# A decoder layer on one Trainium2 core: the order of work at the start of cross-attention, on three engines

## The chip, the cores and the metric

The kernel runs on 1 core of a Trainium2 chip. A core has five engines with queues of their own, each in order: TensorE (PE; its weight loads are shown apart as PEld), VectorE (DVE), ScalarE (ACT), GpSimd (POOL) and SyncE (SP), which here only issues DMAs. ScalarE issues a few DMAs too. Engines wait for each other on semaphores alone. The metric is the device time of one execution in microseconds; lower is better.

## The reference

32 sequences of 128 tokens with 128 features pass a state-space mixer, cross-attention with 16 heads of 8 features over a context of 128 tokens, and a mixture of 16 experts, each with a residual sum and a layer norm behind it. The change touches the start of the middle part:

```python
x = _layernorm(x + mixer(x))
q, k, v = split_heads(x @ Wq + bq), split_heads(ctx @ Wk + bk), split_heads(ctx @ Wv + bv)
scores = einsum('bhqd,bhkd->bhqk', q, k) / sqrt(8)
scores = where(mask, -1e15, scores)
attn = softmax(scores)
x = _layernorm(x + merge(einsum('bhqk,bhkd->bhqd', attn, v)) @ Wo + bo)
x = _layernorm(experts(x))
```

## The kernel before

The sequences are worked in 8 groups of 4. The mixer, attention and the experts are three blocks of straight code per engine; between mixer and attention each engine jumps into the next block by itself, after all have arrived there. Everything in a block is ordered by hand: each engine's function is a list of steps, and each step begins with its semaphore waits.

Attention of one group needs the scores twice. First `scores` makes them by query on TensorE (banks SS0 and SS1), VectorE takes the maximum of each row (`maxima`), splits the negated maxima into three bf16 parts (`split_maxima`, four small operations, L1367 to L1373), TensorE transposes them (`max_rows`, L1563, into bank PO), ScalarE copies them out and stores them to DRAM (`store_max`, L1261 and L1265), and loads them back as extra rows of the stacked queries (`stack_max`, L1271). Then `scoresT` makes the transposed scores with the maxima subtracted (banks TT0 and TT1), ScalarE takes the exponential (`exps`, L1253), and `weigh` multiplies by the values and by ones. `both(g, ..., b, ..., p)` is the steady pair of steps: transposed scores of group g and first scores of group g + 1, for sequence b and half p of the heads. In `both` the transposed scores of a half group wait for its stacked maxima (`d_m`), and each first-score step waits for VectorE's maxima of the turn before it (`v_max`), since the banks are used again.

Group 0 has no group before it, so its first scores are made ahead of the loop by `first_scores`, for sequences 0 to 3 and p 0 and 1; these use TT0 and TT1 as well, and VectorE's `first_maxima` reads them. Both halves of group 0's maxima are transposed there by `max_rows(0, 0)` and `max_rows(0, 1)`.

Around this the next groups are prepared. For group 2: ScalarE rounds the context (`context_hi`, L196), GpSimd takes the rest (L1184), TensorE projects keys (`k_proj`, L254) and transposes x1 (`x1T`, L245), ScalarE evicts (`part_first`, L219, and `x1T_hi`), VectorE takes the rests (`part_rest`, L232, and `x1T_lo`, L212), TensorE projects queries (`q_proj`, L254), and GpSimd makes the third parts (`part_third`, L239). SyncE stores the parts to DRAM and loads them back as stacked rows (`store_parts`, `stacks`). The first scores of group 2 wait for those stacks.

The layer norm of the mixer's last group also falls here: VectorE's `statistics` (L131 and L135, four each), then GpSimd's `normalise_pool` (L141 to L148), then `biased(0)` (L1189). GpSimd does these ahead of its `head(0, ...)`, which holds the mask casts (L1179) and `part_third` of group 2. SyncE waits for that norm before it goes on to `loads(3)` and `store_parts(2)`.

Of the kernel before, what the change touches and what calls it, by code (L numbers as in the profile page):

```python
# [25 lines left out]
GS = 4  # L26
# [271 lines left out]
def mixer(nc, t, d, psum, a):  # L298

    with ExitStack() as ctx:  # L300
# [3 lines left out]
        def sem(name, n=1, by=1):  # L304
            return Sem(ctx, nc, name, n, by)
# [21 lines left out]
        half_dt = sb("half_dt", [P, NSEQ, HEADS])  # L327
        th = sb("th", [P, NSEQ, ROT])

        w_loaded, const = sem("w_loaded", 1, 16), sem("const")  # L330
        wprep = sem("wprep")


        expo = sb("expo", [P, 2, HEADS, P])
# [724 lines left out]
def attention(nc, t, d, psum, a, e):  # L1059
# [12 lines left out]
    with ExitStack() as ctx:  # L1072
# [172 lines left out]
        def _(act):  # L1245
# [10 lines left out]
            def store_max(g, par, half):  # L1256

                act.wait_ge(p_mt.sem, p_mt.at(g, half))
                act.wait_ge(d_ms[half].sem[1 - par], d_ms[half].at(g - 1, 1 - par))
                tok = slice(half * 2 * P, half * 2 * P + 2 * P)  # L1260
                act.activation(nmT[:, tok], PO[:, :].bitcast(BF16)[0:48, tok], ACT.Copy).then_inc(a_mt.sem, 1)  # L1261
                act.wait_ge(a_mt.sem, a_mt.at(g, half))
                act.sem_inc(act_passed, 1)
                act.wait_ge(d_m[half].sem[par], d_m[half].at(g - 2, par))
                act.dma_start(m_dram[par, half], nmT[:, tok]).then_inc(d_ms[half].sem[par], 16)  # L1265
# [54 lines left out]
            for b in range(GS):  # L1320
                act.activation(mask[:, 1, b, :, :].rearrange("p k t -> p (k t)"),
                               mask8[:, 1, b * KINDS * P:(b + 1) * KINDS * P], ACT.Copy).then_inc(g_mask.sem, 1)
            store_max(0, 0, 0)
            context_hi(act, a, 2, 0)
            stack_max(0, 0, 0)
            store_max(0, 0, 1)
            ahead(act, group)

# [1 line left out]
        def _(dve):  # L1330
# [55 lines left out]
            def head(g, par, left, before=None):  # L1386
# [6 lines left out]
                    part_rest(dve, a, g + 2, 1, PF)  # L1393
                if left:
                    maxima(g + 1, 0, (2, 3))
                if left >= 2:
                    x1T_lo(dve, a, g + 2, PO)
                if left:
# [48 lines left out]
            values(0, 0, U0)  # L1447
            dve.wait_ge(g_init, 10)
            values(1, 1, PF)
            statistics(dve, NG - 1, t["x1_res"], dve_passed, res, stats, mv)  # L1450
            head(0, 0, 4)
            dve.wait_ge(x1_out.sem, x1_out.at(NG - 1, 3))
            ahead(dve, group)
# [2 lines left out]
        def _(pe):  # L1456
# [171 lines left out]
            for b in range(2):  # L1628
                for p in range(2):
                    first_scores(b, p)  # L1630
            project_v(pe, t, a, 1, PF)
            max_rows(0, 0, (t["x1_res"].sem, t["x1_res"].at(NG - 1, 0)))
            stacked(0, 0, 1)
            for b in range(2, GS):
                for p in range(2):
                    first_scores(b, p)
            max_rows(0, 1, (a_mt.sem, a_mt.at(0, 0)))
            pe.wait_ge(g_init, 9)
            both(0, 0, 0, 4, 0)
            head_parts(0, 0, 4)  # L1640
            both(0, 0, 0, 4, 1)
            for g in range(NG):
# [497 lines left out]
```

## Time and profile before

| what | us |
| --- | --- |
| median of 3 runs | 602.16 (601.14 to 604.1) |
| the profiled execution, its own time | 599.92 |
| its span from first to last instruction | 598.2 |
| TensorE busy | 545.5 (91% of the span) |
| VectorE busy | 445.2 (74%) |
| ScalarE busy | 280.1 (47%) |
| GpSimd busy | 229.1 (38%) |
| mixer block ends, first attention scores start | 203.0, 207.3 |
| attention's loop, about | 228 to 404 |

A timeline row gives the start and the duration in microseconds, the engine, the line of the kernel, the operation with the tile it writes and those it reads, how many instructions were merged, and in brackets how long the engine had been idle before it and who ended that. ACTq and SPq are the queues that issue DMAs. The clock column of a table of stretches is the TensorE clock that was granted, as a share of 2.4 GHz.

### The profile page before, as it was taken

How to read it: one execution, taken by the hardware profiler on the slowest of the kernel's cores; microseconds unless marked ns; L12 is line 12 of the kernel's file. 1: busy time of each engine (PE TensorE's matmuls, PEld its weight loads, DVE VectorE, ACT ScalarE, POOL GpSimd, SP SyncE). 2: the span in 40 equal slices, each digit the busy share in tenths (PEclk: the TensorE clock that was granted, in tenths of full speed). 3: DMA queues.
4: the chain of work that ended last, by engine and by line, in shares of the span. 5: the costliest groups of instructions: out<-in, count | busy, mean ns of one | idle time of the engine just before them, and what ended most of it. 6: DMA issues, size and time to landing. Idle time of an engine off the chain costs nothing. (4 is left out here: it accounts for less than half of the span.)

```text
span 598.2 us, 17812 instructions
## 1 busy us (share of the span) xinstructions
PE 545.5 (91%) x6344; PEld 452.9 (76%) x6344; DVE 445.2 (74%) x1080; ACT 280.1 (47%) x556; POOL 229.1 (38%) x273
## 2 busy tenths in 40 slices
PE   5769999999999669999999999878999999999994
PEld 5748877787788547878778777767888888888883
DVE  3857877877798487778778787665796887877963
ACT  2358647756675316556556455533323323233220
POOL 2233546534753665244543546713022032131122
PEclk9979999999999958999999999998999999999998
DMA  7124232312332762654654455007246265165160
GB/s 217 38 99 124 76 97 75 122 53 90 102 119 65 200 184 77 185 143 128 173 149 122 136 142 168 7 5 177 65 115 143 63 150 132 60 164 128 38 157 18
DMA packets 55217, 67.42 MB, mean 113 GB/s; under 512 B 6705, under 2 KB 33104, under 8 KB 55152
## 3 DMA queue, kind: packets, MB, share of 16 engines
q1 hardware_dynamic: 52976, 63.58, 39.3%
q0 software_dynamic: 704, 1.92, 1.1%
q10 hardware_dynamic: 1472, 1.05, 0.8%
q8 instruction: 41, 0.67, 0.5%
q14 instruction: 24, 0.20, 0.1%
HBM read 49.26 MB, written 11.21 MB: 101 GB/s over the span
## 5 line engine op out<-in xcount | busy, mean ns | idle before, releaser
L1253 ACT ACTIVATE prob<-bank 128x512 f32<-128x512 f32 x128 | 69.4, 595 | 41.1 <-PE bank L1499 34.8
L2031 PE MATMUL bank<-xT_hl_c,w_up 128*128 128x512 f32 x288 | 85.9, 422 | 2.9 <-ACTq L67 2.9
L1948 ACT ACTIVATE sg<-bank 128x512 f32<-128x512 f32 x72 | 43.1, 598 | 95.2 <-PE bank L2031 89.7
L1349 DVE TENSOR_REDUCE nmax<-bank 128x4 f32<-128x512 f32 x112 | 71.9, 684 | 20.6 <-PE bank L1499 19.3
L2042 PEld LDWEIGHTS bank<-w_down,hid 128*128 128x128 f32 x576 | 73.9, 191 | 10.8 <-DVE hid L1988 3.7
L2042 PE MATMUL bank<-w_down,hid 128*128 128x128 f32 x576 | 76.4, 276 | 2.4 <-DVE res L124 1.5
L1489 PE MATMUL bank<-neg_i,mask 64*128 64x256 bf16 x512 | 52.1, 283 | 12.8 <-DMA q_stack<-q_scratch 4.3
L2031 PEld LDWEIGHTS bank<-xT_hl_c,w_up 128*128 128x128 f32 x288 | 50.2, 194 | 10.0 <-issue 3.1
L1988 DVE TENSOR_TENSOR hid<-gu,share 128x512 f32<-128x512 f32 x64 | 48.9, 763 | 6.0 <-DMA share<-cw_scratch 3.7
L1984 DVE TENSOR_TENSOR gu<-sg,bank_pair 128x512 f32<-128x512 f32 x48 | 32.8, 684 | 19.2 <-ACT sg L1948 13.2
L1747 POOL TENSOR_TENSOR xT_hl_c<-rest,xT_hl_c 128x512 fp32r<-128x512 f32 x7 | 9.0, 1285 | 94.4 <-ACT xT_hl_c L1728 94.4
L491 ACT ACTIVATE expo<-rows,neg_sums 128x128 f32<-128x128 f32 x128 | 40.7, 390 | 9.1 <-DVE mix L913 9.1
L141 POOL TENSOR_TENSOR rstd<-mv,norm_c 128x4 f32<-128x4 f32 x24 | 5.2, 216 | 99.9 <-DVE mv L135 60.1
L820 POOL TENSOR_TENSOR w_tok<-w_tok,prev 128x512 f32<-128x512 f32 x16 | 22.4, 1401 | 52.0 <-DMA prev<-xnext 42.2
L2031 PE MATMUL bank_pair<-xT_hl_c,w_up 128*128 128x512 f32 x144 | 41.1, 394 | 0.0
L1489 PEld LDWEIGHTS bank<-neg_i,mask 64*128 64x128 bf16 x512 | 16.8, 96 | 27.9 <-issue 13.2
L1543 PE MATMUL bank_pair<-prob,v_d 128*32 128x128 f32 x1024 | 34.4, 275 | 0.0
L1539 PE MATMUL bank_pair<-prob,ones_s 128*32 128x128 f32 x1024 | 34.4, 276 | 0.0
L436 PE MATMUL bank<-xhl,w_feat 128*128 128x512 f32 (+1 forms) x96 | 28.2, 429 | 5.3 <-DVE b_rot L869 5.2
L983 PE MATMUL bank_pair<-plain 96*128 96x256 f32 x192 | 29.4, 289 | 3.0 <-DVE mix L913 2.9
L2031 PEld LDWEIGHTS bank_pair<-xT_hl_c,w_up 128*128 128x128 f32 x144 | 27.1, 188 | 6.4
L983 PEld LDWEIGHTS bank_pair<-plain 96*128 96x128 f32 x192 | 25.3, 189 | 8.0 <-DVE mix L913 7.6
(217 smaller groups left out, 1175.2 us busy)
## 6 DMA issues: line engine op xcount, KB each, us to landing
share<-cw_scratch SPq DMA_DIRECT2D x64, 256.0 KB, 5.5
rows<-sum_rows_scratch SPq DMA_DIRECT2D x32, 256.0 KB, 3.5
k_stack<-k_scratch SPq DMA_DIRECT2D x32, 128.0 KB, 2.8
q_stack<-q_scratch SPq DMA_DIRECT2D x32, 128.0 KB, 2.9
prev<-xnext SPq DMA_DIRECT2D x16, 224.0 KB, 2.5
k_scratch<-k_part SPq DMA_DIRECT2D x16, 192.0 KB, 2.4
q_scratch<-q_part SPq DMA_DIRECT2D x16, 192.0 KB, 2.5
x<-xT_in SPq DMA_DIRECT2D x8, 256.0 KB, 8.6
```

Of the source, the lines that this page charges most:

```text
L491: act.activation(expo[:, b % 2, h, :], rows[:, b, h, :], ACT.Exp, bias=upto_s[:, bass.ds(g * GS + b, 1), h]).then_inc(s_exp.sem, 1)
L983: pe.matmul(bank[:, 0:2 * P], plain[:, par, 0, a, tok], bc(plain[:, par, 1, v, None, tok], [PLAIN, 2, P]), start=(n == 0), stop=False, ski ...
L1253: act.activation(prob[:, b % 2, ORDER[n], :, :], (TT0, TT1)[n % 2][:, :], ACT.Exp, scale=XD ** -0.5)\
L1349: dve.tensor_reduce(nmax[:, b, 4 * u:4 * u + 4], (SS0, SS1)[n % 2][:, :].rearrange("p (i k) -> p i k", i=4), AX_X, ALU.max, negate=True).t ...
L1489: pe.matmul(banks[j][:, :].rearrange("p (i h k) -> p i h k", i=4, h=2)[:, :, half, :], mask[rows, par, b, kind + ver, :], bc(neg_i[rows, N ...
L1539: mm = pe.matmul(U1[32 * u:32 * u + 32, 0:P], ones_s[:, 4 * b + i, :, :].rearrange("p r c -> p (r c)"), prob[:, b % 2, u, i, :], start=(b ...
L1543: mm = pe.matmul(U0[32 * u:32 * u + 32, b * P:(b + 1) * P], v_d[:, par, b, i * P + 32 * u:i * P + 32 * u + 32], prob[:, b % 2, u, i, :], s ...
L1948: act.activation(sg[:, k, :], GG[k][:, :], ACT.Silu).then_inc(a_s.sem, 1)
L1984: dve.tensor_tensor(dst, sg[:, k, :], UU[k][:, :], ALU.mult).then_inc(v_gu.sem, 1)
L1988: dve.tensor_tensor(hid[:, c, :], gu[:, k, :], share[:, c - 1, :], ALU.mult).then_inc(v_hid.sem, 1)
L2031: mm = pe.matmul(bank[:, :], w_up[:, which, a, c, :], xT_hl[par][:, v, :], start=(n == 0), stop=(n == 2))
L2042: mm = pe.matmul(PO[:, b * P:(b + 1) * P], hid[:, c, b * P:(b + 1) * P], w_down[:, c, :], start=(c == 0 and b == 0), stop=(c == NC - 1), s ...
```

## The change

Three engines' lists are reordered at the start of attention, and one step is moved on VectorE. No work is added or taken away. (Three semaphores of the mixer that nothing used are dropped as well, so that lines from there on are numbered two lower.)

- TensorE: `first_scores(2, 0)`, with the wait for the second half's stacks, goes ahead of `max_rows(0, 0)`. `max_rows(0, 1)` goes from ahead of `both(0, ..., 0)` to behind it. Ahead of `both` stands a wait for all 16 of group 0's maxima, which the wait in `max_rows(0, 1)` held before.
- ScalarE: `stack_max(0, 0, 0)` goes ahead of `context_hi(2)`.
- VectorE: `statistics` of the mixer's last group goes from ahead of `head(0, ...)` into it, behind the second pair of group 1's maxima and ahead of `x1T_lo(2)`.

```diff
--- before.py
+++ after.py
@@ -327,8 +327,6 @@
         half_dt = sb("half_dt", [P, NSEQ, HEADS])
         th = sb("th", [P, NSEQ, ROT])
 
-        w_loaded, const = sem("w_loaded", 1, 16), sem("const")
-        wprep = sem("wprep")
 
 
         expo = sb("expo", [P, 2, HEADS, P])
@@ -1321,8 +1319,8 @@
                 act.activation(mask[:, 1, b, :, :].rearrange("p k t -> p (k t)"),
                                mask8[:, 1, b * KINDS * P:(b + 1) * KINDS * P], ACT.Copy).then_inc(g_mask.sem, 1)
             store_max(0, 0, 0)
+            stack_max(0, 0, 0)
             context_hi(act, a, 2, 0)
-            stack_max(0, 0, 0)
             store_max(0, 0, 1)
             ahead(act, group)
 
@@ -1393,6 +1391,8 @@
                     part_rest(dve, a, g + 2, 1, PF)
                 if left:
                     maxima(g + 1, 0, (2, 3))
+                if not before:
+                    statistics(dve, NG - 1, t["x1_res"], dve_passed, res, stats, mv)
                 if left >= 2:
                     x1T_lo(dve, a, g + 2, PO)
                 if left:
@@ -1447,7 +1447,6 @@
             values(0, 0, U0)
             dve.wait_ge(g_init, 10)
             values(1, 1, PF)
-            statistics(dve, NG - 1, t["x1_res"], dve_passed, res, stats, mv)
             head(0, 0, 4)
             dve.wait_ge(x1_out.sem, x1_out.at(NG - 1, 3))
             ahead(dve, group)
@@ -1629,14 +1628,15 @@
                 for p in range(2):
                     first_scores(b, p)
             project_v(pe, t, a, 1, PF)
+            stacked(0, 0, 1)
+            first_scores(2, 0)
             max_rows(0, 0, (t["x1_res"].sem, t["x1_res"].at(NG - 1, 0)))
-            stacked(0, 0, 1)
-            for b in range(2, GS):
-                for p in range(2):
-                    first_scores(b, p)
-            max_rows(0, 1, (a_mt.sem, a_mt.at(0, 0)))
+            for b, p in ((2, 1), (3, 0), (3, 1)):
+                first_scores(b, p)
+            pe.wait_ge(v_max.sem, v_max.at(0, 4 * GS - 1))
             pe.wait_ge(g_init, 9)
             both(0, 0, 0, 4, 0)
+            max_rows(0, 1, (a_mt.sem, a_mt.at(0, 0)))
             head_parts(0, 0, 4)
             both(0, 0, 0, 4, 1)
             for g in range(NG):
```

TensorE's queue around the first transposes of maxima. L260 is the product of values (`project_v`); a row of L1489 and one of L1499 with k_stack first are a turn of first scores, with q_stack first a turn of transposed scores; L1563 is `max_rows`. Before:

```order
L260 MATMUL bank<-w_v,cin 128x128 x4
L1563 MATMUL bank<-ident,npart 48x128 x2
L1489 MATMUL bank<-neg_i,mask 128x4x64 x4
L1499 MATMUL bank<-k_stack,q_stack 128x128 x8
L1489 MATMUL bank<-neg_i,mask 128x4x64 x4
```

and in the changed kernel, where those lines are 1488, 1498 and 1562:

```order
L260 MATMUL bank<-w_v,cin 128x128 x4
L1488 MATMUL bank<-neg_i,mask 128x4x64 x4
L1498 MATMUL bank<-k_stack,q_stack 128x128 x8
L1562 MATMUL bank<-ident,npart 48x128 x2
L1488 MATMUL bank<-neg_i,mask 128x4x64 x4
```

The transposes now stand behind one more turn of first scores.

TensorE's queue some turns later, from the last first scores of group 0 to the second turn of `both`. Before:

```order
L1489 MATMUL bank<-neg_i,mask 128x4x64 x4
L1499 MATMUL bank<-k_stack,q_stack 128x128 x8
L1563 MATMUL bank<-ident,npart 48x128 x2
L1489 MATMUL bank<-neg_i,mask 128x4x64 x4
L1499 MATMUL bank<-q_stack,k_stack 128x128 x8
L1489 MATMUL bank<-neg_i,mask 128x4x64 x4
L1499 MATMUL bank<-k_stack,q_stack 128x128 x8
L254 MATMUL bank<-c_hl,wqk_hl 128x512 x3
L245 MATMUL bank<-ident,x 128x128 x4
L1489 MATMUL bank<-neg_i,mask 128x4x64 x4
```

and in the changed kernel:

```order
L1488 MATMUL bank<-neg_i,mask 128x4x64 x4
L1498 MATMUL bank<-k_stack,q_stack 128x128 x8
L1488 MATMUL bank<-neg_i,mask 128x4x64 x4
L1498 MATMUL bank<-q_stack,k_stack 128x128 x8
L1488 MATMUL bank<-neg_i,mask 128x4x64 x4
L1498 MATMUL bank<-k_stack,q_stack 128x128 x8
L1562 MATMUL bank<-ident,npart 48x128 x2
L254 MATMUL bank<-c_hl,wqk_hl 128x512 x3
L245 MATMUL bank<-ident,x 128x128 x4
L1488 MATMUL bank<-neg_i,mask 128x4x64 x4
```

The transposes of the second half's maxima have moved from ahead of the first turn of `both` to behind it, directly ahead of the keys' projection (L254) and the transposes of x1 (L245).

ScalarE's queue around the stored maxima, with its waits. Before:

```order
L1261 ACTIVATE nmT<-bank 48x256 [waits max_stored0_1,max_mm]
L1265 DMA max_scratch<-nmT 48x256 [waits nmT_ready,max_stacked0_0]
L196 ACTIVATE c_hl<-cin 128x512 [waits k_mm,ctx_in0]
L1271 DMA q_stack<-max_scratch 3x2048 [waits max_stored0_0]
L1271 DMA q_stack<-max_scratch 3x2048
L1261 ACTIVATE nmT<-bank 48x256 [waits max_stored1_1,max_mm]
L1265 DMA max_scratch<-nmT 48x256 [waits nmT_ready,max_stacked1_0]
```

and in the changed kernel:

```order
L1259 ACTIVATE nmT<-bank 48x256 [waits max_stored0_1,max_mm]
L1263 DMA max_scratch<-nmT 48x256 [waits nmT_ready,max_stacked0_0]
L1269 DMA q_stack<-max_scratch 3x2048 [waits max_stored0_0]
L1269 DMA q_stack<-max_scratch 3x2048
L196 ACTIVATE c_hl<-cin 128x512 [waits k_mm,ctx_in0]
L1259 ACTIVATE nmT<-bank 48x256 [waits max_stored1_1,max_mm]
L1263 DMA max_scratch<-nmT 48x256 [waits nmT_ready,max_stacked1_0]
```

The two loads of `stack_max`, which wait for the store of the maxima, now stand ahead of the context's copy (L196). The copy of the second half's maxima (L1261 before, L1259 now) is where it was, ahead of the loop's exponentials.

VectorE's queue from the values of group 1 to the first split of group 1's maxima. Before:

```order
L1341 TENSOR_TENSOR v_d<-bank,b_v 128x4x4x8 x4
L131 BN_STATS stats<-res 128x6 x4
L135 BN_AGGR mv<-stats 128x2 x4
L1349 TENSOR_REDUCE nmax<-bank 128x4 x2
L232 SCALAR_TENSOR_TENSOR rest<-bank,bqk,k_part 128x512
L1349 TENSOR_REDUCE nmax<-bank 128x4 x2
L212 TENSOR_TENSOR xT_hl<-bank,xT_hl 128x512
L1349 TENSOR_REDUCE nmax<-bank 128x4 x4
L1367 SCALAR_TENSOR_TENSOR npart<-nmax 128x4x8
```

and in the changed kernel:

```order
L1339 TENSOR_TENSOR v_d<-bank,b_v 128x4x4x8 x4
L1347 TENSOR_REDUCE nmax<-bank 128x4 x2
L232 SCALAR_TENSOR_TENSOR rest<-bank,bqk,k_part 128x512
L1347 TENSOR_REDUCE nmax<-bank 128x4 x2
L131 BN_STATS stats<-res 128x6 x4
L135 BN_AGGR mv<-stats 128x2 x4
L212 TENSOR_TENSOR xT_hl<-bank,xT_hl 128x512
L1347 TENSOR_REDUCE nmax<-bank 128x4 x4
L1365 SCALAR_TENSOR_TENSOR npart<-nmax 128x4x8
```

The eight operations of `statistics` have moved from ahead of the first pair of maxima to ahead of `x1T_lo` (L212) and the four maxima of sequence 1.

## Rows read from the trace of the kernel before

**Rows 1.** Stretch and length; busy of PE, PEld, DVE, ACT, POOL; clock, DMA, GB/s.

```profile
215.00:230.00 15.00, 9.74 (x111) 7.05 (x111) 12.32 (x33) 4.68 (x9) 8.15 (x10) 0.58 0.41 107
...
260.00:400.00 140.00, 133.25 (x3026) 108.71 (x3024) 105.54 (x269) 77.45 (x149) 69.58 (x80) 1.00 0.43 121
```

**Rows 2.** TensorE's timeline: start, duration (us), line, operation, count [idle before <-releaser].

```profile
222.97 0.38 PE L1563 MATMUL bank<-ident,npart 128*48 128x128 bf16 x2 [3.24 <-DVE npart L1373]
...
223.84 0.61 PE L1489 MATMUL bank<-neg_i,mask 64*128 64x256 bf16 x4 [0.50 <-issue]
...
225.66 1.65 PE L254 MATMUL bank<-c_hl,wqk_hl 128*128 128x512 f32 x3
...
227.90 0.39 PE L1489 MATMUL bank<-neg_i,mask 64*128 64x256 bf16 x4
...
229.80 0.40 PE L1489 MATMUL bank<-neg_i,mask 64*128 64x256 bf16 x4 [0.84 <-ACT prob L1253]
...
232.35 0.38 PE L1489 MATMUL bank<-neg_i,mask 64*128 64x256 bf16 x4
...
237.26 0.38 PE L1489 MATMUL bank<-neg_i,mask 64*128 64x256 bf16 x4
...
247.19 0.40 PE L1489 MATMUL bank<-neg_i,mask 64*128 64x256 bf16 x4 [0.22 <-issue]
```

**Rows 3.** ScalarE's timeline, 215 to 228 us.

```profile
215.68 0.35 ACTq L1265 DMA_DIRECT2D max_scratch<-nmT  x1
...
220.12 0.63 ACT L196 ACTIVATE c_hl<-cin 128x512 fp32r<-128x512 f32 x1 [4.55 <-DMA cin<-ctxT_in]
...
221.53 0.75 ACTq L1271 DMA_DIRECT2D q_stack<-max_scratch  x2
...
223.39 0.38 ACT L1261 ACTIVATE nmT<-bank 48x256 bf16<-48x256 bf16 x1 [2.63 <-PE bank L1563]
...
224.98 1.09 ACT L1253 ACTIVATE prob<-bank 128x512 f32<-128x512 f32 x2 [1.21 <-PE bank L1499]
...
227.44 0.69 ACT L219 ACTIVATE k_part<-bank,bqk 128x512 bf16<-128x512 f32 x1 [1.37 <-PE bank L254]
```

**Rows 4.** DMA issues between 214.8 and 215.8 us: KB each, us to landing.

```profile
max_scratch<-nmT ACTq DMA_DIRECT2D x1, 24.0 KB, 5.8
```

**Rows 5.** VectorE's timeline, 216 to 237 us.

```profile
216.16 4.90 DVE L1357 TENSOR_REDUCE nmax<-bank 128x4 f32<-128x512 f32 x8 [1.53 <-PE bank L1499]
...
224.33 0.86 DVE L131 BATCH_NORM_STATS2 stats<-res 128x6 f32<-128x128 f32 x4
...
228.99 1.29 DVE L1349 TENSOR_REDUCE nmax<-bank 128x4 f32<-128x512 f32 x2
...
230.99 1.29 DVE L1349 TENSOR_REDUCE nmax<-bank 128x4 f32<-128x512 f32 x2
...
234.32 0.19 DVE L1367 SCALAR_TENSOR_TENSOR npart<-nmax 128x32 bf16<-128x32 f32 x1
...
235.90 1.29 DVE L1349 TENSOR_REDUCE nmax<-bank 128x4 f32<-128x512 f32 x2
```

**Rows 6.** GpSimd's timeline, 225 to 239 us.

```profile
225.80 0.20 POOL L141 TENSOR_TENSOR rstd<-mv,norm_c 128x4 f32<-128x4 f32 x1 [3.70 <-DVE mv L135]
...
230.50 0.61 POOL L1179 CAST mask<-mask 128x512 bf16<-128x512 uint8 x1
...
237.21 1.16 POOL L239 TENSOR_TENSOR q_part<-rest,q_part 128x512 bf16<-128x512 f32 x1 [3.31 <-ACT q_part L225]
```

**Rows 7.** VectorE's and GpSimd's timelines where their work overlaps.

```profile
220.84 1.26 POOL L1184 TENSOR_TENSOR c_hl<-cin,c_hl 128x512 fp32r<-128x512 f32 x1 [2.92 <-ACT c_hl L196]
...
221.09 1.06 DVE L1367 SCALAR_TENSOR_TENSOR npart<-nmax 128x32 bf16<-128x32 f32 x1
...
390.46 1.29 POOL L1189 TENSOR_TENSOR xb<-x,b_o 128x512 f32<-128x512 f32 x1
...
390.65 1.13 DVE L1774 TENSOR_TENSOR gsum<-gsum,cross 128x16 f32<-128x16 f32 x1
```

## The prediction

> **What bounds the kernel now.** I read the stretches by stage first. In attention's loop, 260 to 400 us, TensorE is busy for 133.25 of 140 us at full clock [rows 1]: whatever delay TensorE has when it enters the loop is carried to the end, and so is a gain. Between 215 and 230 us it is busy for 9.74 of 15 us, at a mean clock of 0.58, so here it waits, and the question is for what. TensorE's timeline answers: before the transposes of the second maxima (222.97) it idles 3.24 us for VectorE's splits, then 0.50 us before the first turn of `both` (223.84), by a releaser that the profile doesn't name, and 0.84 us for ScalarE's exponentials at 229.80 [rows 2]. The 0.50 is the stacked maxima: ScalarE issued their store at 215.68, it took 5.8 us to land (221.48), and the two loads were issued at 221.53, for 0.75 us [rows 3, 4]. 223.84 is 1.56 us behind the end of that issue. So two chains end within half a microsecond of each other at 223.84: the splits, and the maxima's way through DRAM.
>
> **First scores earlier (TensorE).** VectorE idled 1.53 us before the second eight maxima, which take 4.90 us [rows 5]. With `first_scores(2, 0)` ahead of the transposes it can start about 1.3 us sooner and be done near 220, and the splits near 221. That takes the 3.24 us chain away. It does not move the other chain: the first transposes stand behind a turn that is ready by then, so the store of the maxima is issued at 215.7 as before, into the same DMA traffic, which SyncE issues without waiting for TensorE. I put its landing at 221.5 again. Gain at 223.84: none; bounds -0.5 (the unexplained wait is not the maxima) and +0.1.
>
> **Stack ahead of the context's copy (ScalarE).** The copy ran from 220.12 to 220.75 [rows 3], over 0.7 us before the store landed. It held nothing up. Moved behind the two issues it runs at about 222.3, 2.2 us late; GpSimd's subtraction (1.26 us) [rows 7] is then done near 224.3, still ahead of the keys' projection at 225.66 [rows 2]. Cost 0, gain 0.
>
> **Second transposes behind the first turn.** `both`'s first turn lasts 223.84 to 225.66 [rows 2]. The transposes (0.38 us) now stand behind it, so they end at 226.04 and the projection starts 0.38 us late. Worse is ScalarE: the copy of these maxima and their store stand ahead of the first exponentials. The copy began 0.42 us behind the transposes' start (222.97, 223.39), so now at 226.1; 0.38 for it and about 0.6 for the wait and the issue of its store put the exponentials at 227.1 instead of 224.98 [rows 3]. They last 1.09 us, to 228.2. TensorE's second turn waits for them: 228.25 instead of 227.90. ScalarE then comes to the eviction of the keys at 228.1, not 227.44 [rows 3], and everything behind it, with the next exponentials, is 0.6 us late: the turn of 229.80 starts at 230.4. Sum so far +0.6 us.
>
> **Statistics moved (VectorE).** The maxima of 228.99 follow the eviction, so they run 229.6 to 230.9. Now come the statistics, 1.4 us (from 224.33 to the start of GpSimd at 225.80, less the gap) [rows 5, 6]. Before, they lay in time in which VectorE would have waited; here what follows is needed at once. `x1T_lo` takes 0.7 us (from 230.28 to 230.99), and the next pair of maxima starts at 232.9, not 230.99 [rows 5]. TensorE's turn for the other half of the heads began at 232.35, 0.07 us behind their end [rows 2, 5]: no slack. It starts at 234.2 now. Sum +1.9 us.
>
> **GpSimd behind them.** The norm and the bias sum began at 225.80 and lasted to 230.50 [rows 6], 4.7 us. They now begin at 232.3 and end at 237.0, and GpSimd goes on without a gap: a cast (0.61), the third part of the keys (taken as 1.16, like that of the queries), a cast (0.61), to 239.4. Two things hang on that. The queries' third part was made at 237.21 [rows 6] and could start at 239.4: +2.2 us, and with it the stacks of group 2, for which TensorE already had 0.22 us of idle time at 247.19 [rows 2]. Alone this is little more than the 1.9 us that TensorE has lost anyway. The other is a collision. VectorE's splits of group 1's first maxima ran at 234.32, when GpSimd was idle, 0.19 us each [rows 5]. They come at 236.2 now, in the middle of GpSimd's work. What that does is in the trace [rows 7]: the split of 221.09 lasted 1.06 us, until GpSimd's subtraction (220.84 + 1.26 = 222.10) was over; the sum of 390.65 lasted 1.13 us, until GpSimd's of 390.46 was over at 391.75. A split has two inputs in SBUF and can't run beside such a GpSimd operation. There are four, each waiting for the one before it, so after each one GpSimd's next operation has begun: they go through at 237.0, 237.7, 239.1 and 239.9, and the last is done near 240.1 instead of 237.1. That is 3.1 us. No row shows whether a cast, which reads bytes, blocks as well; if it doesn't, the last is done at 238.9, and it is 1.9 us. Behind the splits stand the queries' rest and the pair of maxima that ran at 235.90 to 237.19; TensorE's turn at 237.26 followed 0.07 us behind them [rows 2, 5]. So that turn is late by 1.9 + 1.9 = 3.8 to 1.9 + 3.1 = 5.0 us. I take 4.4, the middle, since nothing lies nearer to either end. The queries' third part is then late by about the same, so the stacks add nothing.
>
> The Trainium skill's page SBUF — State Buffer, section SBUF: two separate sides, says that VectorE and GpSimd share a port pair under "an exclusive lock, not a bandwidth split", taken by a VectorE operation with two SBUF inputs against a GpSimd one that reads SBUF, for the whole instruction. By that rule a cast reads SBUF and blocks, and the delay would be the upper end, 5.0 us; the two blocked rows agree with it.
>
> **Sum.** -0 + 0.6 + 1.3 + 2.5 = +4.4 us. Against the profiled execution's own 599.92 us that is 604.3; the median of the runs is 2.24 us above it, 602.16, so I say 606.6.
>
> **Rivals.**
> *No collision.* GpSimd's operations have small gaps, and the splits slip through them or come at another moment. Then TensorE's loss is that of the stacks, +2.2 us: 604.4. For it: two blocked examples are few. Against: 7 us of GpSimd work without a gap, and a split that comes 0.8 us before the bias sum ends. 15%.
> *The maxima land early, and it isn't slower.* If the 5.8 us of the store [rows 4] were chance and the store took under 3 us, the loads would be issued at 218.5 and `both` would start at 220.8, 3 us early. Its exponentials, the keys' eviction and the first maxima come about 2.2 us earlier than before, the statistics take 1.1 of it back, and GpSimd's third part of the queries ends 0.9 us early: 601.3, if the splits don't collide, 604.1 if they do; 602.7 between. It decides from where `both` starts before 221.9. Against: the same traffic lies under the store. 12%.
> *The stacks come later still.* SyncE also waits for the norm, so the loads of group 3's context and mask now stand right ahead of the store of group 2's keys. If that store lands as slowly as that of the maxima, 5.8 us [rows 4], 3 us more than the issues behind it cover, and half of that shows, TensorE waits near 247 for 1.7 us more: 608.3. It decides if the keys' parts land after the queries' store has been issued. 8%.
> The clock is a smaller one: if TensorE already had its full clock at 223.84, the first turn would take half of its 1.82 us and about 1 us would come back; that lies in the forecast's range.
>
> **How the numbers follow.** The forecast, with both of its ends and 1 us for the clock and the spread of medians, covers 605.2 to 607.8 and has 52%. With the rivals' 15, 12 and 8% this leaves 13% for what I don't see, on both sides. The range from 602.3 to 608.5 leaves out part of the second rival, part of the third and most of the rest, 2 in 10. A measurement here tells about 0.5% from no change, 3.0 us. Slower by more: nearly all of the forecast, the third rival, a third of the rest: 0.60. Within: the other two rivals and a part of the rest: 0.34. Faster by more: 0.06.
>
> **What would show it.** Right: `both`'s first transposed scores still start 16 to 17 us after the first scores; ScalarE's first exponentials come 3 us behind them instead of 1.1; GpSimd's norm starts behind a pair of group 1's maxima; a split of group 1 lasts 0.5 us or more; the turn of 237.26 shows idle time for VectorE; the loop behind is as long as before. Wrong: the store of the first maxima lands within 3 us; all splits last 0.19 us; or the loss of the start is given back in the loop.

## The result, and the profile after

The changed kernel takes 604.94 us (median of 15 runs, 602.18 to 610.91) against 602.16 us for the kernel before (599.13 to 604.1, 15 runs). The ratio is 1.0062, with a 95% interval from 1.0037 to 1.0088: it is slower by 3.7 us (2.2 to 5.3). The forecast was +4.4 us. The profiled executions have spans of 602.3 and 598.2 us.

TensorE's waits from 225 to 400 us in the changed kernel (engine and line, released by; us in total, times, longest):

```profile
PE bank L1488 <- DVE nmax L1347: 4.0, 5, 2.1
PE bank L1488 <- ACT prob L1251: 2.6, 7, 0.9
```

and in the kernel before:

```profile
PE bank L1489 <- ACT prob L1253: 2.8, 6, 0.9
...
PE bank L1489 <- DVE nmax L1349: 0.6, 2, 0.4
```

The waits for VectorE's maxima have grown from 0.6 to 4.0 us, 3.4 us more. Those for ScalarE's exponentials are nearly as they were. Three of these waits, 3.36 us together, stand in TensorE's timeline (columns as in [rows 2]):

```profile
222.24 0.61 PE L1488 MATMUL bank<-neg_i,mask 64*128 64x256 bf16 x4 [5.34 <-DMA q_stack<-max_scratch]
...
229.13 0.39 PE L1488 MATMUL bank<-neg_i,mask 64*128 64x256 bf16 x4 [0.41 <-ACT prob L1251]
...
230.10 0.39 PE L1488 MATMUL bank<-neg_i,mask 64*128 64x256 bf16 x4 [0.35 <-DVE nmax L1347]
...
233.17 0.39 PE L1488 MATMUL bank<-neg_i,mask 64*128 64x256 bf16 x4 [0.89 <-DVE nmax L1347]
...
240.38 0.39 PE L1488 MATMUL bank<-neg_i,mask 64*128 64x256 bf16 x4 [2.12 <-DVE nmax L1347]
...
250.07 0.40 PE L1488 MATMUL bank<-neg_i,mask 64*128 64x256 bf16 x4
```

These answer [rows 2]. The attention block began about 1.0 us earlier in this execution (VectorE's first rest of the queries, L232, at 205.70, against 206.73 in the kernel before), so I count from there. The first turn of `both` starts at 16.54 us from it, where it was 17.11, behind 5.34 us of idle time that the profile now puts down to the stacked maxima by name. The turn that was at 232.35 is at 233.17 with 0.89 us of idle time for VectorE: 27.47 against 25.62, 1.85 us late. The turn that was at 237.26 is at 240.38 with 2.12 us of idle time: 34.68 against 30.53, 4.15 us late. The first scores of group 2, with the stacks, come at 250.07: 44.37 against 40.46, 3.91 us late.

VectorE's timeline in the changed kernel, against [rows 5]:

```profile
224.14 1.29 DVE L1347 TENSOR_REDUCE nmax<-bank 128x4 f32<-128x512 f32 x2 [3.04 <-PE bank L1498]
227.37 0.75 DVE L232 SCALAR_TENSOR_TENSOR rest<-bank,bqk,k_part 128x512 f32<-128x512 f32 x1 [1.94 <-ACT k_part L219]
...
229.96 0.86 DVE L131 BATCH_NORM_STATS2 stats<-res 128x6 f32<-128x128 f32 x4
...
231.83 1.28 DVE L1347 TENSOR_REDUCE nmax<-bank 128x4 f32<-128x512 f32 x2
233.82 1.29 DVE L1347 TENSOR_REDUCE nmax<-bank 128x4 f32<-128x512 f32 x2 [0.71 <-PE bank L1498]
235.14 1.09 DVE L1365 SCALAR_TENSOR_TENSOR npart<-nmax 128x32 bf16<-128x32 f32 x1
236.27 0.52 DVE L1367 TENSOR_TENSOR nrest<-nmax,npart 128x32 f32<-128x32 f32 x1
236.82 1.10 DVE L1369 SCALAR_TENSOR_TENSOR npart<-nrest 128x32 bf16<-128x32 f32 x1
237.95 0.52 DVE L1371 SCALAR_TENSOR_TENSOR npart<-nrest,npart 128x32 bf16<-128x32 f32 x1
238.39 0.74 DVE L232 SCALAR_TENSOR_TENSOR rest<-bank,bqk,q_part 128x512 f32<-128x512 f32 x1
239.05 1.27 DVE L1347 TENSOR_REDUCE nmax<-bank 128x4 f32<-128x512 f32 x2
```

and GpSimd's timeline there, against [rows 6]:

```profile
231.42 0.20 POOL L141 TENSOR_TENSOR rstd<-mv,norm_c 128x4 f32<-128x4 f32 x1 [10.58 <-DVE mv L135]
...
234.91 1.27 POOL L1187 TENSOR_TENSOR xb<-x,b_o 128x512 f32<-128x512 f32 x1
236.13 0.61 POOL L1177 CAST mask<-mask 128x512 bf16<-128x512 uint8 x1
236.70 1.17 POOL L239 TENSOR_TENSOR k_part<-rest,k_part 128x512 bf16<-128x512 f32 x1
237.80 0.61 POOL L1177 CAST mask<-mask 128x512 bf16<-128x512 uint8 x1
239.87 1.16 POOL L239 TENSOR_TENSOR q_part<-rest,q_part 128x512 bf16<-128x512 f32 x1 [1.45 <-ACT q_part L225]
```

The four splits start at 235.14 and are done at 238.47, 3.33 us instead of 0.87. Laid beside GpSimd's rows each one ends just behind one of GpSimd's operations: the bias sum (234.91 + 1.27 = 236.18) and the split until 236.23; the cast (until 236.74) and the split until 236.79; the keys' third part (until 237.87) and the split until 237.92; the cast (until 238.41) and the split until 238.47. The statistics themselves run at 229.96, and VectorE has no gap from 228.75 until 233; the 3.0 us in which it could have had them for nothing are the gap ahead of 224.14.

ScalarE's timeline in the changed kernel, against [rows 3]:

```profile
214.45 0.35 ACTq L1263 DMA_DIRECT2D max_scratch<-nmT  x1
218.00 0.76 ACTq L1269 DMA_DIRECT2D q_stack<-max_scratch  x2
218.86 0.63 ACT L196 ACTIVATE c_hl<-cin 128x512 fp32r<-128x512 f32 x1 [4.51 <-DMA q_stack<-max_scratch]
224.50 0.38 ACT L1259 ACTIVATE nmT<-bank 48x256 bf16<-48x256 bf16 x1 [5.01 <-PE bank L1562]
...
225.59 1.08 ACT L1251 ACTIVATE prob<-bank 128x512 f32<-128x512 f32 x2 [0.71 <-ACT nmT L1259]
226.56 0.69 ACT L219 ACTIVATE k_part<-bank,bqk 128x512 bf16<-128x512 f32 x1
```

and the store of its first maxima among the DMA issues (KB each, us to landing), against [rows 4]:

```profile
max_scratch<-nmT ACTq DMA_DIRECT2D x1, 24.0 KB, 3.5
```

Here the forecast's conclusion held, but by two errors that cancelled. The store landed after 3.5 us, not 5.8. But the two loads behind it, issued at 218.00, let TensorE go only at 222.24, 3.5 us behind the end of their issue, where it had been 1.56. The two trips together took from 214.45 to 222.24, 7.8 us; before, from 215.68 to 223.84, 8.2 us.

### The profile page after: what moved, and what is told of

The parts are those of the page before. It is cut to its first block and busy times, and to the rows that moved or that the text cites. A ratio compares the mean times of both kernels' runs of the same rounds, so it can differ in the third digit from the quotient of the medians.

```text
span 602.3 us, 17813 instructions
## 1 busy us (share of the span) xinstructions
PE 546.3 (91%) x6344; PEld 452.9 (75%) x6344; DVE 444.7 (74%) x1080; ACT 280.1 (47%) x556; POOL 229.6 (38%) x273
```

## The experiments

Runs of one kernel spread over 0.8% and more (599.13 to 604.1 us for the kernel before), and single parts of this change are worth less than that. So each kernel was also read in its profile at four places of TensorE's timeline, counted in us from the start of VectorE's first rest of the queries (L232, the row at 206.73 in the kernel before). The columns are: the first turn of `both`; the score turn that was at 232.35; the one that was at 237.26; the first scores of group 2; and the four splits of group 1's first maxima, from the start of the first to the end of the last. Each ratio is against runs of the kernel before taken beside that kernel; their median lay between 602.16 and 604.89 us from one comparison to the next, so the ratios are compared below and not the bare medians. b_norm_wait has 4 runs of its own, x_gate 8, the others 10 to 15. The places are read from one profile of each kernel.

| kernel | first turn | 232.35's | 237.26's | group 2's | splits | ratio to before (95%) |
| --- | --- | --- | --- | --- | --- | --- |
| before | 17.11 | 25.62 | 30.53 | 40.46 | 0.87 | 1 |
| changed | 16.54 | 27.47 | 34.68 | 44.37 | 3.33 | 1.0062 (1.0037 to 1.0088) |
| a_stats_old | 16.40 | 25.99 | 30.88 | 40.98 | 0.87 | 0.9976 (0.9949 to 1.0003) |
| b_stats_new | 17.57 | 28.17 | 35.38 | 44.91 | 3.33 | 1.0058 (1.0030 to 1.0086) |
| a_first_act | 16.93 | 25.49 | 30.40 | 40.60 | 0.87 | 0.9989 (0.9958 to 1.0019) |
| b_pool_late | 17.40 | 26.34 | 33.30 | 42.84 | 3.08 | 1.0021 (0.9988 to 1.0054) |
| a_stats_mid | 15.75 | 25.61 | 30.50 | 40.35 | 0.87 | 1.0007 (0.9983 to 1.0031) |
| b_second | 17.38 | 26.53 | 31.44 | 41.04 | 0.87 | 1.0005 (0.9977 to 1.0033) |
| b_norm_wait | 16.53 | 25.23 | 30.14 | 45.54 | 0.87 | 1.0104 (1.0033 to 1.0174) |
| b_act | 15.53 | 24.44 | 29.35 | 39.75 | 0.87 | 1.0011 (0.9970 to 1.0053) |
| a_gate | 14.38 | 25.32 | 32.53 | 42.17 | 3.33 | 1.0026 (1.0005 to 1.0048) |
| x_gate | 14.49 | 24.02 | 28.93 | 39.14 | 0.87 | 0.9962 (0.9946 to 0.9979) |

### The statistics back at their old place (a_stats_old)

```diff
             values(1, 1, PF)
+            statistics(dve, NG - 1, t["x1_res"], dve_passed, res, stats, mv)
             head(0, 0, 4)
...
                 if left:
                     maxima(g + 1, 0, (2, 3))
-                if not before:
-                    statistics(dve, NG - 1, t["x1_res"], dve_passed, res, stats, mv)
```

> The changed kernel with the statistics of the mixer's last group back at their old place on VectorE, ahead of group 1's first maxima. Theory (the statistics' place is nearly the whole loss, through the maxima that they hold up and through GpSimd's late work, which collides with the splits): no idle time for VectorE ahead of the score turn that waited 2.12 us, all splits of group 1 at 0.19 us, and the time within 0.5 us of the kernel before (ratio 0.999 to 1.001). Rival (the second transposes behind the first turn of both, by the late exponentials, cost as much): 1.5 us or more above the kernel before.

Measured: ratio 0.9976 (0.9949 to 1.0003), a little under the 0.999 to 1.001 expected, though its interval reaches it. It is not slower than the kernel before, and it is 0.9% under the changed kernel by the two ratios. The splits are at 0.19 us each again, the turn of 237.26 comes at 30.88 instead of 34.68. What is left of the delay behind the first turn is 9.59 us to the second column against 8.51 before: 1.1 us for the second transposes and for the clock (below), partly paid for by the 0.7 us by which the first turn is earlier. The statistics' place is the loss.

### The statistics' move alone (b_stats_new)

```diff
             values(1, 1, PF)
-            statistics(dve, NG - 1, t["x1_res"], dve_passed, res, stats, mv)
             head(0, 0, 4)
...
                 if left:
                     maxima(g + 1, 0, (2, 3))
+                if not before:
+                    statistics(dve, NG - 1, t["x1_res"], dve_passed, res, stats, mv)
```

> The kernel before with the statistics' move alone. Theory: the score turn at 232.35 is 1.3 to 1.5 us late, the splits of group 1's first maxima last 3.3 us together instead of 0.87, the turn at 237.26 is 3.8 us late, and the time is 3.3 to 4.3 us above the kernel before. Rival (the move only hurts together with the transposes' move, which makes VectorE late already): under 1.5 us.

Measured: ratio 1.0058 (3.5 us, where 3.3 to 4.3 were expected), as much as the whole change. At the two places the delay is larger than expected: the turn of 232.35 is 2.55 us late instead of 1.3 to 1.5, the one of 237.26 4.85 us instead of 3.8. The first turn is 0.46 us late already, and TensorE's clock stays at 1.2 GHz for longer than in the kernel before (last section). Its splits, in VectorE's timeline:

```profile
237.83 1.09 DVE L1367 SCALAR_TENSOR_TENSOR npart<-nmax 128x32 bf16<-128x32 f32 x1
238.96 0.52 DVE L1369 TENSOR_TENSOR nrest<-nmax,npart 128x32 f32<-128x32 f32 x1
239.51 1.09 DVE L1371 SCALAR_TENSOR_TENSOR npart<-nrest 128x32 bf16<-128x32 f32 x1
240.64 0.52 DVE L1373 SCALAR_TENSOR_TENSOR npart<-nrest,npart 128x32 bf16<-128x32 f32 x1
```

1.09, 0.52, 1.09 and 0.52 us, the pattern of the changed kernel. The statistics' move does its harm without the other parts of the change.

### GpSimd late, VectorE untouched (b_pool_late)

```diff
             context_lo(2, 0)
+            pool.wait_ge(v_max.sem, v_max.at(1, 3))
             normalise_pool(pool, NG - 1, t["x1_res"], x1_out, res, mv, rstd, norm_c, x1[:, NSEQ - GS:, :])
```

> The kernel before, statistics at their old place, with one more wait on GpSimd: the mixer's last norm starts behind group 1's first four maxima, about 230.3 instead of 225.8. VectorE has not an instruction more in its way. Theory (the collision of GpSimd's late work with the splits is the larger half of the loss): the four splits last 3.0 to 3.4 us together instead of 0.87, the turn at 237.26 is 2.3 to 2.6 us late, the time 2.3 to 2.8 us above the kernel before. Rival (the loss is VectorE's own occupancy by the statistics, or the stacks): at most 0.5 us above it, since the queries' third part is made at 237.4, 0.2 us later than now.

The ratio, 1.0021 (0.9988 to 1.0054), holds both the theory's 2.3 us and no change; the trace decides. The splits last 3.08 us. The turn of 237.26 is 2.77 us late, where 2.3 to 2.6 were expected, but 0.72 us of that are there at the second column already. Between the second and the third column lie 6.96 us where the kernel before has 4.91: 2.05 us for the splits. TensorE's row there:

```profile
239.71 0.39 PE L1490 MATMUL bank<-neg_i,mask 64*128 64x256 bf16 x4 [1.91 <-DVE nmax L1350]
```

1.91 us of idle time for VectorE's maxima, in a kernel in which VectorE has exactly the instructions of before in the order of before. So GpSimd's lateness delays that turn, by the splits; that it costs as much of the whole time is not shown by the runs.

### The statistics one pair of maxima earlier (a_stats_mid)

```diff
                 if left:
                     maxima(g + 1, 0, (0, 1))
+                if not before:
+                    statistics(dve, NG - 1, t["x1_res"], dve_passed, res, stats, mv)
...
                 if left:
                     maxima(g + 1, 0, (2, 3))
-                if not before:
-                    statistics(dve, NG - 1, t["x1_res"], dve_passed, res, stats, mv)
```

> The changed kernel with the statistics one pair of maxima and one rest earlier: behind group 1's first pair of maxima, where VectorE idled 1.94 us for ScalarE. Theory (it is the place, not the move, that costs): VectorE's later work is not late, GpSimd's norm starts about 4.5 us earlier than in the changed kernel and is through its norm and bias before the splits, of which at most one is blocked; the time is 0 to 1 us above the kernel before. Rival (any place behind group 1's first maxima costs the same 4 us): 3 us or more above it.

Measured: 1.0007 (0.9983 to 1.0031), all splits at 0.19 us, the third column at 30.50. From the first turn to the third column it is 14.75 us, against 14.48 in a_stats_old. GpSimd's norm starts 20.32 us from the mark instead of 25.72 in the changed kernel, 5.4 us earlier for a move by two steps (4.5 were expected), since the rest of the keys between them waits for ScalarE. Inside the same function two steps earlier the statistics cost 0.3 us at most in the trace.

### The second transposes alone (b_second)

```diff
-            max_rows(0, 1, (a_mt.sem, a_mt.at(0, 0)))
+            pe.wait_ge(v_max.sem, v_max.at(0, 4 * GS - 1))
             pe.wait_ge(g_init, 9)
             both(0, 0, 0, 4, 0)
+            max_rows(0, 1, (a_mt.sem, a_mt.at(0, 0)))
```

> The kernel before with the second transposes alone moved behind the first turn of both. Theory: the first exponentials come 3.2 to 3.4 us behind the start of that turn instead of 1.1, the second and third turns are 0.3 to 0.6 us late, nothing else changes: 0.3 to 0.6 us above the kernel before. Rival (it helps, since the first turn no longer stands behind the splits): both starts 0.5 us earlier or more and the time is under that of the kernel before.

Measured: 1.0005 with an interval of 0.3% to either side, so the time says nothing about half a microsecond. In the trace the first exponentials come 3.36 us behind the first turn (1.14 before), TensorE then waits for ScalarE twice (its timeline, the first three turns of transposed scores):

```profile
224.51 0.61 PE L1489 MATMUL bank<-neg_i,mask 64*128 64x256 bf16 x4 [4.38 <-DMA q_stack<-max_scratch]
...
229.01 0.39 PE L1489 MATMUL bank<-neg_i,mask 64*128 64x256 bf16 x4 [0.36 <-ACT prob L1253]
...
231.14 0.39 PE L1489 MATMUL bank<-neg_i,mask 64*128 64x256 bf16 x4 [1.07 <-ACT prob L1253]
```

0.36 and 1.07 us (no wait, and 0.84, before). From the first turn to the second column it is 9.15 us instead of 8.51, 0.64 us, just above the 0.3 to 0.6 expected. The first turn did not start sooner; its 4.38 us of idle time are now put down to the stacked maxima.

### ScalarE's order alone (b_act)

```diff
             store_max(0, 0, 0)
+            stack_max(0, 0, 0)
             context_hi(act, a, 2, 0)
-            stack_max(0, 0, 0)
             store_max(0, 0, 1)
```

> The kernel before with ScalarE's order alone changed: the loads of the stacked maxima ahead of the context's copy. Theory: nothing, within 0.5 us of the kernel before; both starts as before if the store lands behind the context, up to 1 us earlier if it lands ahead of it. Rival (the late copy holds the keys' projection): 0.5 us or more above it, with idle time ahead of the projection put down to GpSimd.

Ratio 1.0011 (0.9970 to 1.0053): inconclusive at this size. In this one execution the store landed after 3.4 us, ahead of the context, and the first turn started 1.6 us earlier than in the kernel before, more than the 1 us expected. The keys' projection did not wait for the late copy. The first turn stood right behind the second transposes there, with no idle time between them, so what bound it was VectorE's splits; and the first of these, at 219.27, lasted 1.30 us, to the end of GpSimd's subtraction (219.26 + 1.26). With one profile, and the store's landing differing by itself from 3.4 to 6.4 us between kernels, I can't tell how much of the 1.6 us is the order's.

### The first turn and ScalarE's order, without the two later moves (a_first_act)

```diff
             max_rows(0, 0, (t["x1_res"].sem, t["x1_res"].at(NG - 1, 0)))
             for b, p in ((2, 1), (3, 0), (3, 1)):
                 first_scores(b, p)
-            pe.wait_ge(v_max.sem, v_max.at(0, 4 * GS - 1))
+            max_rows(0, 1, (a_mt.sem, a_mt.at(0, 0)))
             pe.wait_ge(g_init, 9)
             both(0, 0, 0, 4, 0)
-            max_rows(0, 1, (a_mt.sem, a_mt.at(0, 0)))
```

with the statistics at their old place as above.

> The changed kernel without the statistics' move and without the second transposes' move: left are the earlier turn of first scores and ScalarE's stacking ahead of the context copy. Theory: both starts 0 to 0.6 us earlier, bound by the stacked maxima; the exponentials are not held up, so that gain is kept: 0 to 0.6 us under the kernel before. Rival (the moves of the front are worth the 1.5 us by which VectorE ends sooner): 1.3 us or more under it.

Measured: first turn at 16.93, 0.18 us earlier than before, third column 0.13 us earlier, ratio 0.9989 (0.9958 to 1.0019). VectorE ended group 0's splits 2.1 us sooner (at 14.01 instead of 16.09 from the mark), and TensorE turned it into a wait (its timeline, the second transposes and the first turn):

```profile
220.72 0.38 PE L1561 MATMUL bank<-ident,npart 128*48 128x128 bf16 x2 [2.37 <-DVE npart L1371]
223.49 0.61 PE L1487 MATMUL bank<-neg_i,mask 64*128 64x256 bf16 x4 [2.39 <-issue]
```

2.39 us idle where there were 0.50. The time gained on VectorE's chain is not worth anything as long as the maxima's way through DRAM ends where it does.

### A gate on the transfers beside the maxima (x_gate and a_gate)

SyncE issues the mask of group 2 and the second half of group 1's stacks while the maxima are under way, and neither is needed soon. Both kernels hold them until the stacked maxima have landed:

```diff
             stacks(1, 1, 0)
-            loads(2, 0)
+            sp.wait_ge(p_v.sem, p_v.at(0))
+            sp.dma_start(cin[:, 0, :], d["ctxT"][:, bass.ds(2 * GT, GT)]).then_inc(d_c.sem[0], 16)
+            sp.wait_ge(d_m[0].sem[0], d_m[0].at(0, 0))
+            sp.wait_ge(g_mask.sem, g_mask.at(0, GS - 1))
+            sp.dma_start(mask8[:, 0, :].bitcast(mybir.dt.int32), d["mask"][:, bass.ds(2 * GT, GT)])\
+                .then_inc(d_mask.sem[0], 16)
             stacks(1, 1, 1)
```

x_gate is a_first_act with it, a_gate the changed kernel with it.

> The changed kernel with the statistics and the second transposes at their old places, and on SyncE a gate: the mask of group 2 and the second half of group 1's stacks are issued only when the first stacked maxima have landed. Theory (the start of the first transposed scores is bound by the maxima's two trips through DRAM, which are slow because of the transfers beside them): the store lands in 2 to 3 us instead of 5.7, the loads in under 2.5 us, both starts 2 to 2.5 us earlier than in the kernel before, and this is kept: ratio 0.996 or 2 to 2.5 us less. Rival (the trips have a fixed cost of this size, or VectorE's maxima bind next): less than 1 us earlier, ratio 0.999.

> The changed kernel as it is, with the same gate on SyncE. Theory (GpSimd's late work and the statistics cost what they cost from wherever the start lies): both starts 2 us earlier, the four splits still last 2 us or more together, the loss between the first transposed scores and the queries' stacks is 3 to 4 us as in the changed kernel, and the time is about 4 us above that of the gated kernel without the two moves. Rival (an early start moves the splits out of GpSimd's way): the splits last 0.87 us and the time is within 2 us of it.

x_gate: 600.1 us, ratio 0.9962 (0.9946 to 0.9979), 2.3 us under the kernel before. The first turn starts at 14.49, 2.6 us earlier. The store took 3.4 us, a little over the 2 to 3 expected; the loads let TensorE go 1.5 us behind the end of their issue. It is the loads that the gate shortened: the store took 3.5, 3.5 and 3.4 us in the changed kernel, a_stats_old and a_stats_mid as well, without a gate, but there the loads let TensorE go only 3.5, 3.3 and 3.0 us behind the end of their issue. In a_gate it is 3.7 us for the store and 1.65 us for the loads. The store and the loads in ScalarE's timeline of x_gate:

```profile
214.51 0.35 ACTq L1268 DMA_DIRECT2D max_scratch<-nmT  x1
217.93 0.74 ACTq L1274 DMA_DIRECT2D q_stack<-max_scratch  x2
```

and the first turn of `both` and two later ones in TensorE's:

```profile
220.17 0.61 PE L1492 MATMUL bank<-neg_i,mask 64*128 64x256 bf16 x4 [0.49 <-issue]
...
226.71 0.39 PE L1492 MATMUL bank<-neg_i,mask 64*128 64x256 bf16 x4 [0.41 <-ACT prob L1256]
...
227.69 0.39 PE L1492 MATMUL bank<-neg_i,mask 64*128 64x256 bf16 x4 [0.35 <-DVE nmax L1352]
```

Of the 2.6 us 1.6 are left at the second and third column and 1.3 at group 2's scores. The turns of 226.71 and 227.69 wait 0.41 and 0.35 us, and the ones ahead ran at half clock for longer (last section). It is the one kernel here whose whole interval lies under the kernel before.

a_gate: ratio 1.0026 (1.0005 to 1.0048). It starts as early, at 14.38, and its splits last 3.33 us all the same. From the first turn to group 2's scores it takes 27.79 us, against 24.65 in x_gate: 3.1 us more, inside the expected 3 to 4. By the two ratios the difference is 0.64%, 3.9 us. The two kernels differ in the second transposes' place too, not in the statistics' alone. So the loss doesn't hang on where the start lies, and the early start that was the second rival's condition does not get the splits out of the way.

### The norm behind the splits (b_norm_wait)

```diff
             context_lo(2, 0)
+            pool.wait_ge(v_split.sem, v_split.at(1, 3))
             normalise_pool(pool, NG - 1, t["x1_res"], x1_out, res, mv, rstd, norm_c, x1[:, NSEQ - GS:, :])
```

> The kernel before with the mixer's last norm on GpSimd held until VectorE has split group 1's first maxima, so that nothing collides, but the norm starts at about 28.5 us behind the attention's first query rest instead of 19.1. Theory (the splits' collision is what held the turn at 237.26; the stacks are a second chain with little slack): the splits last 0.87 us, that turn shows no idle time, the queries' third part is made 5 us late, at 35.6 instead of 30.5, and the first scores of group 2 wait 4 to 5 us for their stacks: 4 to 5 us above the kernel before. Rival (the stacks have slack, and the loss in the changed kernel had nothing of them): under 1 us.

Ratio 1.0104 (1.0033 to 1.0174), 6.3 us from four runs, where 4 to 5 were expected and the interval goes from 2.0 to 10.5. The norm starts at 28.15, the splits last 0.87 us, and the third column is at 30.14: no loss there. Then TensorE waits twice, in its timeline:

```profile
243.31 0.39 PE L1490 MATMUL bank<-neg_i,mask 64*128 64x256 bf16 x4 [2.92 <-ACT prob L1254]
...
251.94 0.39 PE L1490 MATMUL bank<-neg_i,mask 64*128 64x256 bf16 x4 [1.25 <-issue]
```

The second wait, 1.25 us, I put down to the stacks of group 2, for which 4 to 5 us were expected; the profile names no releaser. The first, 2.92 us, I had not expected: it is put down to ScalarE's exponentials. SyncE loads the context of group 3 only behind this norm, and ScalarE's copy of that context stands ahead of exponentials in its queue. ScalarE's timeline shows the copy waiting for that load:

```profile
241.66 0.63 ACT L196 ACTIVATE c_hl<-cin 128x512 fp32r<-128x512 f32 x1 [3.58 <-DMA cin<-ctxT_in]
```

Together the first scores of group 2 come 5.1 us late (45.54 against 40.46). So a late norm has three ways to reach TensorE: the splits, the stacks and the next context.

## Why the prediction was right, and where its sizes were off

The forecast was 606.6 us, slower, in a range from 602.3 to 608.5; measured were 604.94 and a ratio worth 3.7 us. The mechanism is the forecast's. That the sum came so near is partly luck: the first turn gave back 0.57 us that the forecast had not counted, and the step behind it cost 0.5 us more than its term. The terms compare like this, on the way to the turn of 237.26:

| step | forecast, us | measured, us | from |
| --- | --- | --- | --- |
| start of the first turn | 0 (-0.5 to +0.1) | -0.57 | changed kernel |
| second transposes behind it | +0.6 | +1.1 with the clock, +0.64 alone | a_stats_old, b_second |
| statistics on VectorE | +1.3 | +1.3 | 10.93 less 9.59 us, changed kernel and a_stats_old |
| splits against GpSimd | +2.5 (1.9 to 3.1) | +2.3 | 7.21 less 4.91 us, changed kernel and before |
| sum at that turn | +4.4 | +4.15 | |

- **First scores earlier: nearly right, by two numbers that were wrong.** VectorE was done 2 us sooner and TensorE idled 5.34 us for the maxima. The store's 5.8 us was read as its fixed price in this traffic; it was 3.5 us here, and the loads took most of the rest (3.5 us behind their issue instead of 1.56). The first turn came at 15.5 to 17.6 us from the mark in the ten kernels without the gate and at 14.4 and 14.5 us in the two with it, so SyncE's transfers have a part in it; what places it within those 2 us is open.
- **Stack ahead of the context's copy: no loss, right.** That it gains nothing is not shown: b_act started 1.6 us sooner in its one profile.
- **Second transposes: right in kind.** The exponentials come 3.35 us behind the first turn (225.59 less 222.24), expected were about 3.3. The half microsecond missing in the term is the clock as far as the rows go, which I had listed as a possible gain. It was a loss: x_gate, with neither of the two later moves but with a clock that came back late, takes 9.53 us from the first turn to the second column, where a_first_act takes 8.56. The late clock doesn't hang on the transposes' move, since b_stats_new has it too.
- **Statistics: right**, to 0.1 us, where changed kernel and a_stats_old are compared. From the kernel before to b_stats_new the same stretch grows by 2.09 us (10.60 less 8.51), with the later clock in it; how much of that is the clock's isn't separated.
- **Collision: right.** Four splits, each held by GpSimd's next operation, as laid out. The choice between the ends was open for want of a row with a cast. The casts block: the splits of 236.27 and 237.95 last 0.52 us, each to the end of a cast. The Trainium skill's page SBUF — State Buffer, section SBUF: two separate sides, says that the lock holds against a GpSimd operation that reads SBUF, and these two casts agree. The upper end was still not reached, so that the middle I took was near for a reason that I had not seen: I had counted 0.2 us for each split between two of GpSimd's operations, but these follow one another without a gap (234.91, 236.13, 236.70, 237.80) and the splits' own time lies beside them.
- **The stacks add nothing: right.** Group 2's scores are 3.91 us late, less than the turn before them.
- **The sum against the measured time.** 4.15 us at the turn, 3.91 at group 2, 4.1 in the spans, 3.7 by the ratio. The loop behind is not the fixed length I took it for: from group 2's scores to the last output product of attention (L1570) it lasted from 153.6 to 159.5 us between the kernels of this study, 153.8 before and 154.3 in the changed kernel. A single profile carries that length with it: x_gate's, with a loop of 157.5 us, ends its attention later than the kernel before does (197 against 194 us from the mark, at the last L1570's start), while its runs are faster. The medians are 2.8 us apart. So the totals here are the ratios', and the profiles are used for the places ahead of the loop alone. Why the loop's length differs, beyond TensorE's waits for stacks and stacked maxima in it, is left open.

Of the rivals, *no collision* fell to the splits' rows. *The maxima land early* came near in its first step only: the store landed after 3.5 us, not under 3, and the loads took most of that back. a_gate shows that with a start 2.7 us earlier than in the kernel before the splits still collide. *The stacks come later still* didn't happen; b_norm_wait shows what it looks like when the norm is later by another 2.4 us.

## What to carry to other kernels

A step moved off an engine that has no time for it has to be followed through the engines behind it: these 1.3 us of statistics cost 1.3 us on VectorE, and 2.3 us more because GpSimd's work behind them came to lie over four tiny VectorE operations. Look where small operations with two inputs in SBUF stand, and keep the other engine's long elementwise work away from that stretch; two steps earlier the same statistics cost 0.3 us at most. And when two chains end together, shortening the one that the profile names turns into a wait for the other: here it was a store and a load through DRAM, and the turn behind them came 2.4 to 2.6 us earlier (x_gate against a_first_act and against the kernel before) by holding back transfers that nobody needed yet.

## What the runs showed of the hardware

- **A chain of small VectorE operations loses to GpSimd at each link.** Operations of 0.19 us lasted 1.09, 0.52, 1.10 and 0.52 us in the changed kernel and nearly the same in b_stats_new and a_gate. GpSimd is hardly slowed by it (its keys' third part lasted 1.17 us, the queries' 1.16 us). A cast from bytes holds VectorE's split as an addition does; the maxima, which read PSUM, were not held: the pair at 233.82 took 1.29 us beside GpSimd's work, as ever.
- **A small store takes from 3.4 to 6.4 us in traffic.** The 24 KB of the first maxima landed in 3.4 to 3.7 us in six kernels and in 4.7 to 6.4 us in six others, including kernels with the same order on SyncE and ScalarE. The store of 238.27 in b_norm_wait, as large and with hardly any other transfer under way at its start, landed after 1.4 us.
- **The clock came back later in the changed kernel, and differently from kernel to kernel.** The table of stretches of the changed kernel (columns as in [rows 1]):

```profile
227.50:228.00 0.50, 0.50 (x12) 0.44 (x8) 0.50 (x1) 0.34 (x2) 0.00 (x0) 0.50 0.00 0
228.00:228.50 0.50, 0.50 (x12) 0.39 (x8) 0.12 (x1) 0.50 (x2) 0.00 (x0) 0.50 0.00 0
228.50:229.00 0.50, 0.22 (x6) 0.00 (x0) 0.25 (x1) 0.48 (x1) 0.00 (x0) 0.71 0.00 0
```

and of the kernel before:

```profile
227.00:227.50 0.50, 0.50 (x3) 0.39 (x2) 0.03 (x1) 0.06 (x1) 0.43 (x1) 0.50 0.00 0
227.50:228.00 0.50, 0.50 (x6) 0.33 (x6) 0.00 (x0) 0.50 (x1) 0.50 (x1) 0.88 0.00 0
```

In the kernel before the granted clock rises between 227.5 and 228, 3.7 to 4.2 us behind the start of unbroken work at 223.84. In the changed kernel work is unbroken from 222.24 and the clock stays at 1.2 GHz until past 228.5, 6.3 us. What went ahead differs: in the kernel before TensorE was at 1.2 GHz through all of group 0's first scores; in the changed one it stood at 2.4 GHz from 215 on, kept that into its 5.34 us of idle time, and was back at 1.2 GHz from 219. x_gate is like the changed kernel (2.4 GHz until about 220, work from 220.17, 2.4 GHz again past 226.5), and a_first_act like the one before (1.2 GHz throughout, work from 223.49, 2.4 GHz from about 227.3). But this makes no rule. b_act and b_norm_wait had also stood at 2.4 GHz for a while and had it back 4.8 and 4.3 us behind the start of the first turn, and b_pool_late, at 1.2 GHz throughout, only after 4.8 us. What decides it stays open. I had weighed a clock that is up already at the start, and not one that comes back 2 us later.
